# Post-LN linear attention and FFN on 8 cores: weight loads of the first stage through two slots, and the Wq and Wo casts placed among the key/value chunks

## What is computed

```python
q = _phi(heads(x @ Wq.T + bq))            # _phi(y) = elu(y) + 1
k = _phi(heads(x @ Wk.T + bk))
v = heads(x @ Wv.T + bv)
kv = jnp.einsum('bhtd,bhtm->bhdm', k, v)
z = 1.0 / (jnp.einsum('bhtd,bhd->bht', q, k.sum(axis=2) + EPS) + EPS)
out = jnp.einsum('bhtd,bhdm,bht->bhtm', q, kv, z)
attn = out.reshape(Bq, Tq, -1) @ Wo.T + bo
x = _layernorm(x + attn)
h = silu(x @ wg.T) * (x @ wu.T)           # wg, wu, wd = int32 / 127
x = _layernorm(x + h @ wd.T)
```

## Time and profile before

| what | value |
|---|---|
| runs of the kernel before | 4986.19 and 5011.02 us, median 4998.6 |
| the profiled execution's own time | 4986.74 us |
| its span, slowest core (core 4) | 4985.2 us |
| spans of all cores | 4970.2 to 4985.2 us |
| TensorE matmul busy | 3624.7 us, 73% |
| VectorE busy | 1682.7 us, 34% |
| ScalarE busy | 1161.0 us, 23% |
| GpSimd busy | 272.3 us, 5% |
| mean granted TensorE clock, by core | 0.853 to 0.856 |

### The profile page before, as it was taken

The page is one execution under the profiler, slowest core; times in us unless marked ns, Lnnn a source line. Parts: engine busy times, 40 slices in busy tenths (PEclk is TensorE's granted clock), DMA queues, the critical chain, the costliest instruction groups (busy, mean ns, idle before and its releaser), DMA issues.

```text
span 4985.2 us, 43788 instructions; the slowest of 8 cores (4970.2 to 4985.2 us)
## 1 busy us (share of the span) xinstructions
PE 3624.7 (73%) x14893; PEld 1440.6 (29%) x15184; DVE 1682.7 (34%) x2435; ACT 1161.0 (23%) x2043; POOL 272.3 (5%) x284
## 2 busy tenths in 40 slices
PE   1587746666774877699983877699983877699992
PEld 0232212222321322244431322244430322244440
DVE  0123422222233134433343134433334124333334
ACT  2233421111112243311112243311112233311112
POOL 0001000000011001000001001000001000100002
PEclk9797768888886987899996987799996987799996
DMA  5100022222213000010003000001003000001001
GB/s 160 45 0 1 1 76 76 76 76 64 66 37 119 1 1 1 26 48 29 35 17 135 0 1 1 26 26 51 26 26 135 1 1 1 26 26 51 26 26 68
DMA packets 69679, 200.02 MB, mean 40 GB/s; under 512 B 4933, under 2 KB 4934, under 8 KB 60248
## 3 DMA queue, kind: packets, MB, share of 16 engines
q1 hardware_dynamic: 56504, 153.15, 8.8%
q10 hardware_dynamic: 12960, 44.05, 2.6%
HBM read 144.75 MB, written 52.43 MB: 40 GB/s over the span
## 4 chain that ended last, share of the span: by engine, by line
PE 61%; DVE 13%; ACT 8%; DMA 8%; issue 6%; POOL 4%; DVEq 0%; ACTq 0%; SPq 0%; POOLq 0%; another core or an unknown queue 0%
PE ps L779 13%; PE ps L758 12%; PE ps L804 12%; PE ps L420 5%; PE ps L626 5%; PE ps L374 4%; DVE wstage L254 4%; DVE x L258 4%; PE ps L535 3%; DMA wstage_i<-wu 3%; POOL arena L192 2%; DMA wstage_i<-wg 2%; DVE h_arena L790 2%; POOL h_arena L192 1%; ACT arena L592 1%
## 5 line engine op out<-in xcount | busy, mean ns | idle before, releaser
L758 PE MATMUL ps<-y_bf,arena 128*128 128x512 bf16 x3012 | 709.8, 389 | 183.4 <-POOL arena L727 72.6
L779 PE MATMUL ps<-y_bf,arena 128*128 128x512 bf16 x3008 | 701.0, 387 | 113.4 <-DVE arena L727 109.9
L804 PE MATMUL ps<-h_arena,arena 128*128 128x512 bf16 x3012 | 692.0, 379 | 39.1 <-DVE h_arena L790 36.1
L768 ACT ACTIVATE h_arena<-ps 128x512 bf16<-128x512 f32 x384 | 229.2, 597 | 1868.3 <-PE ps L758 1868.2
L790 DVE SCALAR_TENSOR_TENSOR h_arena<-ps,h_arena 128x512 bf16<-128x512 f32 x384 | 265.6, 692 | 1046.2 <-PE ps L779 1043.1
L816 DVE SCALAR_TENSOR_TENSOR x<-ps,x 128x512 f32<-128x512 f32 x768 | 530.3, 692 | 184.2 <-PE ps L804 98.1
L420 PE MATMUL ps<-wk_bf,arena 128*128 128x512 bf16 x993 | 283.8, 431 | 300.8 <-ACT arena L445 177.8
L758 PEld LDWEIGHTS ps<-y_bf,arena 128*128 128x128 bf16 x3072 | 305.2, 100 | 575.2 <-issue 235.7
L779 PEld LDWEIGHTS ps<-y_bf,arena 128*128 128x128 bf16 x3072 | 303.7, 99 | 495.6 <-issue 151.4
L804 PEld LDWEIGHTS ps<-h_arena,arena 128*128 128x128 bf16 x3072 | 294.0, 98 | 421.5 <-issue 85.4
L192 POOL TENSOR_TENSOR arena<-x 128x512 bf16<-128x512 f32 x160 | 164.1, 1038 | 3990.2 <-DVE x L634 1989.3
(11 more groups left out here) (78 smaller groups left out, 2357.5 us busy)
## 6 DMA issues: line engine op xcount, KB each, us to landing
x<-x SPq DMA_DIRECT2D x16, 2048.0 KB, 8.0
out<-x SPq DMA_DIRECT2D x16, 2048.0 KB, 7.8
arena<-stash_wg SPq DMA_DIRECT2D x18, 1024.0 KB, 4.8
arena<-stash_wd SPq DMA_DIRECT2D x18, 1024.0 KB, 7.0
arena<-stash_wu ACTq DMA_DIRECT2D x18, 1024.0 KB, 4.8
wstage_i<-wg SPq DMA_DIRECT2D x48, 256.0 KB, 2.9
wstage_i<-wd ACTq DMA_DIRECT2D x48, 256.0 KB, 2.7
wstage_i<-wu SPq DMA_DIRECT2D x48, 256.0 KB, 2.7
```

The costliest lines, as they stand in the source:

```text
L758: e.matmul(ps[b_][:, 0:512], slots[sl_][:, 512 * kk + 128 * gg:512 * kk + 128 * (gg + 1)], y_bf[:, T * kk + t_:T * kk + t_ + 512], start=( ...
L779: e.matmul(ps[b_][:, 0:512], slots[sl_][:, 512 * kk + 128 * gg:512 * kk + 128 * (gg + 1)], y_bf[:, T * kk + t_:T * kk + t_ + 512], start=( ...
L804: e.matmul(ps[b_][:, 0:512], slots[sl_][:, 1024 * ss + 128 * mm:1024 * ss + 128 * (mm + 1)], h_arena[:, 512 * ss:512 * (ss + 1)], start=(s ...
```

## The change

Three things are changed, all for the first sequence only.

1. Wk goes through columns 0 to 1023 of `wstage` with semaphore `sqw`, Wv through columns 1045 to 2068 with a semaphore of its own, `svw`. The first loads of both are issued one behind the other; after its cast, each slot's next load is issued at once. ScalarE still issues and casts everything, in the order Wk, Wv.
2. Wq and Wo are no longer cast in the prologue. When all of Wk and Wv is cast, SP issues the first load of each. The casts (`emit_deferred_cast`) are emitted for ScalarE behind the last instruction of a chunk, by a table: one piece of Wq in each of chunks 2 to 9, two pieces of Wo in chunks 10 and 11, and one in each of 12 to 15.
3. The later loads of Wq and Wo are issued by SP, each behind the cast that frees its slot.

```diff
@@ -170,6 +170,7 @@
         slot_sem = [SEM(f"slot{i}") for i in range(4)]
         st_w = SEM("st_w")
         sqw = SEM("sqw")
+        svw = SEM("svw")
         scst = SEM("scst")
         stash_val = {}
         xq_state = {}
@@ -286,21 +287,6 @@
         p.op("vector", lambda e: e.memset(zrow[:], 0.0), inc=dve)
         init_dve = dve.n
         wcast = {}
-        def load_attn_weight(name, wdram, wsb, wcols, qeng, qsem, slot_of,
-                             stage_free):
-            vals = []
-            for c in range(NCH):
-                p.wait(qeng, act, stage_free)
-                p.dma(qeng, qsem, wstage[:, slot_of:slot_of + wcols],
-                      wdram[128 * c:128 * (c + 1), :])
-                p.wait("scalar", qsem, qsem.n)
-                p.op("scalar", lambda e, cc=c, w=wsb, wc=wcols, so_=slot_of:
-                     e.copy(w[:, wc * cc:wc * cc + wc],
-                            wstage[:, so_:so_ + wc]), inc=act)
-                stage_free = act.n
-                vals.append(act.n)
-            wcast[name] = vals
-            return stage_free
 
         def prefetch_x(b):
             st = []
@@ -318,22 +304,60 @@
         prefetch_x(0)
         wcast["wk"] = []
         wcast["wv"] = []
-        sf = bias_ready
-        for c in range(NCH):
-            for wname, wdram, wsb in (("wk", wkt_d, wk_bf), ("wv", wvt_d, wv_bf)):
-                p.wait("scalar", act, sf)
+        p.wait("scalar", act, bias_ready)
+        p.dma("scalar", sqw, wstage[:, 0:D], wkt_d[0:128, :])
+        p.dma("scalar", svw, wstage[:, 1045:1045 + D], wvt_d[0:128, :])
+        for k in range(NCH):
+            p.wait("scalar", sqw, 16 * (k + 1))
+            p.op("scalar", lambda e, kk=k:
+                 e.copy(wk_bf[:, D * kk:D * (kk + 1)], wstage[:, 0:D]),
+                 inc=act)
+            wcast["wk"].append(act.n)
+            if k + 1 < NCH:
+                p.wait("scalar", act, wcast["wk"][k])
                 p.dma("scalar", sqw, wstage[:, 0:D],
-                      wdram[128 * c:128 * (c + 1), :])
-                p.wait("scalar", sqw, sqw.n)
-                p.op("scalar", lambda e, cc=c, w=wsb:
-                     e.copy(w[:, D * cc:D * (cc + 1)], wstage[:, 0:D]), inc=act)
-                sf = act.n
-                wcast[wname].append(act.n)
+                      wkt_d[128 * (k + 1):128 * (k + 2), :])
+            p.wait("scalar", svw, 16 * (k + 1))
+            p.op("scalar", lambda e, kk=k:
+                 e.copy(wv_bf[:, D * kk:D * (kk + 1)],
+                        wstage[:, 1045:1045 + D]), inc=act)
+            wcast["wv"].append(act.n)
+            if k + 1 < NCH:
+                p.wait("scalar", act, wcast["wv"][k])
+                p.dma("scalar", svw, wstage[:, 1045:1045 + D],
+                      wvt_d[128 * (k + 1):128 * (k + 2), :])
         kv_w_ready = act.n
-        sf2 = load_attn_weight("wq", wqt_d, wq_bf, D, "sync", sd, 1045,
-                               bias_ready)
-        load_attn_weight("wo", wot_d, wo_bf, D, "scalar", sqw, 0, sf)
-        qo_ready = act.n
+
+        wcast["wq"] = []
+        wcast["wo"] = []
+        wq_dma = []
+        wo_dma = []
+        p.wait("sync", act, kv_w_ready)
+        p.dma("sync", sd, wstage[:, 1045:1045 + D], wqt_d[0:128, :])
+        wq_dma.append(sd.n)
+        p.dma("sync", sqw, wstage[:, 0:D], wot_d[0:128, :])
+        wo_dma.append(sqw.n)
+        defer_cast = {2: [("wq", 0)], 3: [("wq", 1)], 4: [("wq", 2)],
+                      5: [("wq", 3)], 6: [("wq", 4)], 7: [("wq", 5)],
+                      8: [("wq", 6)], 9: [("wq", 7)],
+                      10: [("wo", 0), ("wo", 1)], 11: [("wo", 2), ("wo", 3)],
+                      12: [("wo", 4)], 13: [("wo", 5)], 14: [("wo", 6)],
+                      15: [("wo", 7)]}
+
+        def emit_deferred_cast(wname, j):
+            qsem, slot, wsb, wdram, dvals = (
+                (sd, 1045, wq_bf, wqt_d, wq_dma) if wname == "wq"
+                else (sqw, 0, wo_bf, wot_d, wo_dma))
+            p.wait("scalar", qsem, dvals[j])
+            p.op("scalar", lambda e, jj=j, w=wsb, so_=slot:
+                 e.copy(w[:, D * jj:D * (jj + 1)], wstage[:, so_:so_ + D]),
+                 inc=act)
+            wcast[wname].append(act.n)
+            if j + 1 < NCH:
+                p.wait("sync", act, wcast[wname][j])
+                p.dma("sync", qsem, wstage[:, slot:slot + D],
+                      wdram[128 * (j + 1):128 * (j + 2), :])
+                dvals.append(qsem.n)
 
         for b in range(BPC):
             xq_loaded = xq_state[b]
@@ -476,6 +500,9 @@
                 if c + 1 < TCH:
                     emit_xc(c + 1)
                 emit_proj_and_evacs(c, prev)
+                if b == 0:
+                    for wname_, j_ in defer_cast.get(c, []):
+                        emit_deferred_cast(wname_, j_)
                 prev = c
             emit_kv(TCH - 1)
 
```

## The result

The changed kernel took 4901.67 us, median of its runs, where 4900 was predicted (range 4878 to 4928). Against the kernel before, 5002.86 us measured beside it, the ratio is 0.9812, 95% interval 0.9796 to 0.9827: 94 us less on a base of about 4995, between 86 and 102. It is faster, and the 2% line lies inside the interval.

What follows compares the result with a forecast made beforehand. Two TensorE waits in the first key/value stage were taken as the bound: 63.7 us behind ScalarE's casts, 80.8 us for Wk. Gains 61.7 + 26.8 + 1.1 = 89.6 from 4986.7 gave 4897, plus 3 for spread: 4900 us, range 4878 to 4928.

Steps and rivals of the forecast that it cites:

- Part A: Wq and Wo casts leave the prologue, so TensorE's chunk 1 starts at 108.60 in place of 170.34: gain 61.7 us.
- Part B: Wk and Wv through two slots: a pair takes 4.49 us instead of 8.97, last Wk cast at 69.0: gain 26.8 us.
- the rival with both slots served: Wk/Wv loads both get served while x lands: 7th lands near 48, 15th at 66, total 4897 us; chance 0.15.
- the lower bound: Wk/Wv loads: two in flight slow each other by 0.8 us a trip over 6 trips, leaving a gain of 22 us.
- The upper bound of 33 us for B: Wk/Wv loads limited only by the DMA engines: last Wk cast about 62 to 64, gain 33 us.
- Part C: TensorE's clock in chunk 1: with only 1.92 us of pause ahead, it lasts 11.81 us, not 12.93: gain 1.1 us.
- Part D: The 16 deferred casts in chunks 2 to 15 fit ScalarE's 5.87 us waits, 0.35 us to spare in 10 and 11: cost nothing.
- Part E: SP's queue: the FFN's first gate weight load leaves later, after the last of Wo, in chunk 14: cost nothing.
- The sum: Whole kernel: 61.7 + 26.8 + 1.1 = 89.6 us off the profiled 4986.7, giving 4897; with 3 us added, 4900.
- the second slot doesn't do what it says: Rival on the Wk/Wv loads: one queue's loads serialise in full, 16 trips remain, total 4922 us; chance 0.07.
- the deferred casts show: Rival on chunks with deferred casts: they delay evacuation and TensorE's next chunk, up to 17 us, total 4914; chance 0.08.
- the low clock: Rival on chunks 1 to 15: TensorE stays at its lower clock level, costing 103 us, total 5000; chance 0.02.

Runs made afterwards that it cites:

- e2_slots_only: The changed kernel with its two slots for Wk and Wv, but all Wq and Wo casts back in the prologue; ratio to the kernel before 0.9948.

## Why the prediction was right

**Part A, 61.7 us.** Right. The run with the casts deferred alone moved chunk 1 by 63.5 us, of which 1.6 are the first Wq load's, as the working had it. The wait of 63.66 us was an order on ScalarE, and the work behind it was late for no other reason.

**Part B, 26.8 us.** The size was right (106.81 - 81.75 = 25.1, and 1.6 for the Wq load), and two of its steps were wrong in opposite directions. "A second load waiting in ScalarE's queue would then not get a turn of its own" is the first: both slots were served while x landed, and the 7th cast started at 47.68 where the 5th was forecast for 46.5. That is the rival with both slots served, in its first half. "One slot's trip stays 4.49 us" is the second: with two in flight it is 5.40, near the lower bound that the prediction worked out from a Wq load beside another one (0.8 a trip; measured 0.91). Two casts more are one trip less (-4.5 us); it was given back by a start 1.2 us later and by 4 x 0.91 = 3.6 us of slower trips. The 7th cast at 47.68 and four trips of 5.40 end at 69.3, the forecast's 5th at 46.5 and five trips of 4.49 at 69.0. That the two agree within 0.3 us is luck: the mechanism while x lands was not the one described, and two errors of about 4 us cancelled.

The upper bound of 33 us for B was false too: eight slots beside x gave an end at 53.76 in place of 95.77, 42 us. It took for granted that x is served first.

The rule of the Trainium skill, "DMA: Bandwidth & Descriptors", section "Queues, rings and completion order", that an engine goes round between the queues a packet at a time, isn't refuted by this. What fell is what was made of it here, that two loads in one queue share one turn and that a turn is a quarter of x: the run with x in eight loads shows no such turn.

**Part C, 1.1 us.** Wrong in size: chunk 1 lasts 94.55 - 81.75 = 12.80 us, against 12.93 before. The step "so it should be one of the mean" failed. Its first eight matmuls took 3.24 us where a group of K at the higher level takes 1.89, and the granted clock from 81 to 85 us was 0.64, although only 1.92 us of pause stand ahead of it (0.50 from 170 to 174 us before). Seven cores have a chunk 1 of 12.6 to 12.8 us; core 1, with the same pause, has a granted clock of 1.00 there and 11.05 us. Gain 0.1 on core 4, 0.5 on the mean of the cores.

**Part D, nothing.** Right, with its margin: 0.32 us behind chunk 11 where 0.35 was worked out, from the start of chunk 15 to the first copy of K^T V (L487 before, L514 now) it is 13.93 us before and after, and the run with four casts shows the price where the cover is gone.

**Part E, nothing.** Right: SP issued the FFN's first load at 249.78, behind the last of Wo at 249.41, long before its first reader on GpSimd at 573.44.

**The sum.** Measured at chunk 1 of core 4: 88.6 us, plus 0.1 for C, where 89.6 was forecast; over the eight cores 89.8 plus 0.5 in the mean. The ratio says 94, with 86 to 102 around it; the profiled execution of the kernel before (4986.7) is among its fastest, and the sum was made against that one. The sum gave 4897; the 3 us added to it are a guess for the spread of executions, and part of why 4900 is so near to 4901.67. The rivals: "the second slot doesn't do what it says" falls by e2_slots_only; "the deferred casts show" by the 1.92 us pauses; the low clock by chunk steps of (247.69 - 94.55) / 13 = 11.78 us after the change, 11.81 before.

## What to carry to other kernels

An engine that works in order makes everything behind a wait as late as the wait: of 89 us, 63 came from moving casts that nobody needed yet to a place where that engine stood idle; whether they cost anything there can be read off from its idle time before the next instruction that someone waits for. Count the staging slots for a load next: here, with x out of the way, a piece took 4.49 us with one slot, 2.72 with two, 1.88 with four and 1.65 with eight, which was the engines' rate. If a large transfer runs at the same time and isn't needed yet, issue it later, and check that a forecast that comes out right does so by its own steps.

## What the runs showed of the hardware

- While SP streams x (DMA engines 0.99 to 1.00 busy, 312 to 321 GB/s), a 512 KB load issued by ScalarE takes, behind the first ones, 7.9 and 8.2 us from issue to cast with one in flight, 7.6 to 8.8 with two (core 4), 7.8 to 9.0 with two and x in 1 MB DMAs (core 0), and 18.8 to 20.1 with eight. The weights' part of the rate grew with the loads in flight: 57, 116 and 206 GB/s with one, two and eight.
- With no x beside it, a load takes 3.2 to 3.6 us alone and 3.8 to 4.9 (mean 4.3) with a second one in flight in the same queue; with the second in the other queue it takes 4.0 to 4.6.
- After the same pause of 1.92 us and about 9 us of matmuls ahead of it, chunk 1 began mostly at the lower level of the clock on core 4 (eight matmuls in 3.24 us, granted clock 0.64) and at the higher one on core 1 (1.89 us, 1.00).
